# Retention outputs and gate kept with channels on partitions in a two-layer transformer kernel

## The reference

```python
xh = x.reshape(B, S, HEADS, HEAD)                 # 16, 256, 8, 16; x is the normalised input
q, k, v = (einsum('bshd,hde->bshe', xh, W) for W in (Wq, Wk, Wv))
scores = einsum('bnhd,bmhd->bhnm', q, k) * D[None]     # causal decay
ret = einsum('bhnm,bmhd->bnhd', scores, v)
mu, var = mean(ret, axis=-1), var(ret, axis=-1)        # over the 16 channels of a head
ret = (ret - mu) * rsqrt(var + EPS)
ret = ret.reshape(B, S, HIDDEN) * gn_w + gn_b
gated = x @ W1
out = (gated * sigmoid(gated) + ret) @ W2
```

## Time and profile before

| what | us |
|---|---|
| median of 3 runs (770.76 to 773.18) | 770.95 |
| the profiled execution | 769.98 |
| its span, first to last instruction | 768.1 |
| PE busy in it | 704.7 (92%) |
| DVE busy | 547.3 (71%) |
| ACT busy | 419.5 (55%) |
| POOL busy | 327.5 (43%) |

### The profile page before, as it was taken

One profiled execution on the slowest core, in us unless ns is written; L12 is line 12 of the kernel. 1 busy time (PEld: TensorE's weight loads), 2 busy tenths in 40 slices (PEclk: granted clock), 3 DMA queues, 4 the chain that ended last, 5 costly groups with the idle time before them and its releaser, 6 DMA issues.

```text
span 768.1 us, 17690 instructions
## 1 busy us (share of the span) xinstructions
PE 704.7 (92%) x6133; PEld 526.7 (69%) x6133; DVE 547.3 (71%) x1053; ACT 419.5 (55%) x802; POOL 327.5 (43%) x433
## 2 busy tenths in 40 slices
PE   5787788998899978979898999999999999999997
PEld 4643445556755537756666888888888888888885
DVE  6878997885688856779886766666666666666665
ACT  5745665776577768667664444444444444444442
POOL 3765644783758860147694641212122222222222
PEclk9999999999999999999999999999999999999999
DMA  6974655431144420011113511112121211211100
GB/s 190 265 231 140 174 149 199 152 103 43 54 127 125 131 84 1 9 36 57 57 44 117 152 55 55 55 41 67 42 68 42 66 43 53 56 51 59 41 15 14
DMA packets 63796, 66.51 MB, mean 87 GB/s; under 512 B 6513, under 2 KB 41841, under 8 KB 63729
## 3 DMA queue, kind: packets, MB, share of 16 engines
q1 hardware_dynamic: 62128, 63.23, 27.5%
q0 software_dynamic: 1024, 2.12, 1.1%
q10 hardware_dynamic: 576, 0.27, 0.1%
HBM read 47.46 MB, written 17.99 MB: 85 GB/s over the span
## 4 chain that ended last, share of the span: by engine, by line
PE 75%; DVE 10%; ACT 5%; issue 4%; DMA 3%; POOL 2%; SPq 0%; ACTq 0%; POOLq 0%; DVEq 0%
PE ps L1763 25%; PE ps L1992 22%; DVE m L1241 3%; PE ps L1876 3%; PE ps L1683 3%; PE ps L1587 3%; DMA qk_parts<-qk_p 2%; PE ps L1796 2%; PE ps L1831 2%; PE ps L1597 2%; PE ps L1593 2%; PE ps L1897 1%; PE ps L1601 1%; PE ps L1688 1%; PE ps L1580 1%
## 5 line engine op out<-in xcount | busy, mean ns | idle before, releaser
L963 ACT ACTIVATE f_h<-ps 128x512 fp32r<-128x512 f32 x256 | 153.3, 599 | 197.7 <-PE ps L1763 197.7
L1463 DVE SCALAR_TENSOR_TENSOR f_l<-ps,f_h 128x512 fp32r<-128x512 f32 x256 | 175.9, 691 | 112.5 <-ACT f_h L963 111.3
L1763 PE MATMUL ps<-x_hl,w_h 128*128 (+1 forms) x512 | 200.3, 391 | 0.0
L783 POOL TENSOR_TENSOR acc<-acc,yt 128x512 f32<-128x512 f32 x55 | 70.9, 1289 | 249.8 <-DVE yt L1501 249.8
L877 ACT ACTIVATE probs<-ps 128x1536 f32<-128x1536 f32 x64 | 92.8, 1450 | 33.9 <-PE ps L1606 33.3
L1763 PEld LDWEIGHTS ps<-x_hl,w_h 128*128 128x128 f32 x512 | 96.1, 188 | 19.6
L682 POOL TENSOR_SCALAR_AFFINE_SELECT probs<-probs 128x512 f32<-128x512 f32 x128 | 78.4, 637 | 59.9 <-ACT probs L877 59.6
L1992 PE MATMUL ps<-f_l,w_h 128*128 128x512 f32 x256 | 99.8, 390 | 1.4 <-DVE f_l L1463 1.4
L1992 PE MATMUL ps<-f_h,w_h 128*128 128x512 f32 x256 | 99.7, 390 | 0.0
L1763 PE MATMUL ps<-x_hl,w_l 128*128 (+1 forms) x256 | 99.6, 389 | 0.0
L1992 PE MATMUL ps<-f_h,w_l 128*128 128x512 f32 x256 | 99.6, 389 | 0.0
(11 more groups left out here) (225 smaller groups left out, 1329.5 us busy)
## 6 DMA issues: line engine op xcount, KB each, us to landing
gate_b<-gate_rows SPq DMA_DIRECT2D x64, 256.0 KB, 3.3
qk_parts<-qk_p SPq DMA_DIRECT2D x16, 512.0 KB, 3.9
k_st<-qk_parts SPq DMA_DIRECT2D x64, 96.0 KB
q_st<-qk_parts SPq DMA_DIRECT2D x64, 96.0 KB
y_tok<-zero SPq DMA_DIRECT2D x8, 512.0 KB, 2.7
w_raw<-in_w_e SPq DMA_DIRECT2D x16, 256.0 KB, 2.8
x_rows<-xn_rows SPq DMA_DIRECT2D x8, 260.0 KB, 4.2
w_up<-in_w_up SPq DMA_DIRECT2D x8, 256.0 KB, 2.9
```

Of the source, the lines that this page charges most:

```text
L783: nc.gpsimd.tensor_tensor(acc[:, :], acc[:, :], yt[:, e % 2, :], ALU.add).then_inc(summed, 1)
L963: nc.scalar.activation(r32(f_h[:, m % 4, :]), ps[:, m % 4, :], ACT.Relu).then_inc(f_hi, 1)
L1463: nc.vector.scalar_tensor_tensor(out=r32(f_l[:, m % 4, :]), in0=ps[:, m % 4, :], scalar=0.0, in1=f_h[:, m % 4, :], op0=ALU.max, op1=ALU.su ...
L1763: last = nc.tensor.matmul(dst, r32(lhs[i]), r32(rhs[j]), start=(k == 0), stop=(k == 2))
```

## The change

Retention outputs stay with channels on partitions all the way from the weighing to W2. ACT makes squares and a copy straight from `ps_o1`. PE sums the squares of a head by a product with a constant 128x128 matrix `same_head` (one where two channels share a head), which leaves each sum in all 16 channels of its head, so root and inverse now run on 128x256. DVE multiplies `o1` by `gn_w` (now one number per partition) and by the inverse in one instruction; POOL adds `sg` and writes `zT`. The transpositions, `ret`, `ss1`, `z`, `put_heads`, `put_turned` and `square_sums` go. For this the gate must have channels on partitions too: in `products` the token-major product shrinks from 264 to 136 columns and a new one, with the gate weights stationary and 256 token columns moving, is added. POOL adds `gn_b` to `sg` once, in 16 instructions. `ps_at1` moves to bank 7. `add_retention` goes ahead of the masks in DVE's step, ACT's root moves between its two score copies, `project1` comes a step earlier (s-3), and the sum of squares of s-2 stands behind the scores. One more constant is loaded at the start (64 KB) and `gn_w` is smaller.

```diff
...
 def ps_qk1(u): return ps[:, 2 + u, :]
-def ps_p1(u, t): return ps[:, 4 + 2 * u + t, 0:PROJ1]
-def p1_both(u): return ps[:, 4 + 2 * u:6 + 2 * u, 0:PROJ1]
+def ps_p1(u): return ps[:, 4 + 2 * u, 0:TB * (D + E)].rearrange("p (t c) -> p t c", t=TB)
+def ps_g1(u): return ps[:, 5 + 2 * u, 0:S]
 ps_o1 = ps[:, 6, 0:S]
-ps_at1 = ps[:, 6, S:2 * S]
-ps_r1 = ps[:, 7, 0:S]
-ps_zt = ps[:, 7, S:2 * S]
+ps_at1 = ps[:, 7, S:2 * S]
+ps_ss1 = ps[:, 7, 0:S]
 EARLY, LATE = slice(0, NT * 3 // 4), slice(NT * 3 // 4, NT)
...
         last.then_inc(v1_here, 1)
+    for b in range(B):
+        pool.wait_ge(sg_put, b + 1)
+        nc.gpsimd.tensor_tensor(sg[:, b, :], sg[:, b, :], gn_b[:, 0:1].broadcast_to([P, S]), ALU.add).then_inc(sg_biased, 1)
     pool.wait_ge(lg1_put, B + CREDIT)
-    pool.wait_ge(sg_put, B)
...
             pool.wait_ge(z_a, b)
-            tiles = z[:, (b - 1) % 2, :, :]
-            nc.gpsimd.tensor_tensor(tiles, tiles, gn_w[:, :].unsqueeze(1).broadcast_to([P, TB, D]), ALU.mult).then_inc(z_b, 1)
-            pool.wait_ge(z_b, b)
-            nc.gpsimd.tensor_tensor(tiles, tiles, sg[:, (b - 1) * TB:b * TB, :], ALU.add).then_inc(z_done, 1)
+            pool.wait_ge(sg_biased, B)
+            if b >= 3:
+                pool.wait_ge(wo_mm, B + b - 2)
+            nc.gpsimd.tensor_tensor(zT[:, (b - 1) % 2, :], o1[:, (b - 1) % 2, :], sg[:, b - 1, :], ALU.add).then_inc(z_done, 1)
         if b % 2 == 1 and b + 1 < B:
...
         act.wait_ge(p1_mm, b + 1 + CREDIT)
-        nc.scalar.activation(sg[:, ds(b * TB, TB), :], p1_both(u)[:, :, D + E:PROJ1], ACT.Silu).then_inc(sg_put, 1)
+        nc.scalar.activation(sg[:, ds(b, 1), :].rearrange("p o t -> p (o t)"), ps_g1(u), ACT.Silu).then_inc(sg_put, 1)
         if isinstance(b, int) and b == 3:
...
         if b >= 1:
-            act.wait_ge(turned1, b)
-        nc.scalar.activation(o1[:, :], ps_o1, ACT.Copy).then_inc(o1_evac, 1)
+            act.wait_ge(squared, b)
+        if b >= 2:
+            act.wait_ge(z_done, b - 1)
+        nc.scalar.activation(sq[:, :], ps_o1, ACT.Square)
+        nc.scalar.activation(o1[:, b % 2, :], ps_o1, ACT.Copy).then_inc(o1_evac, 1)
     def deviation_of(b):
-        act.wait_ge(ss_done, b + 1)
+        act.wait_ge(squared, b + 1)
         if b >= 2:
             act.wait_ge(rden_done, b - 1)
-        nc.scalar.activation(sd1[:, b % 2, :, :], ss1[:, b % 2, :, :], ACT.Sqrt, bias=eps[:, 0:1], scale=1.0 / HD1).then_inc(sd_done, 1)
-    def put_heads(b):
-        act.wait_ge(turned1, b + 1)
-        if b >= 2:
-            act.wait_ge(z_a, b - 1)
-        nc.scalar.activation(ret[:, b % 2, :, :].rearrange("p t c -> p (t c)"), ps_r1, ACT.Copy)
-        if b >= 1:
-            act.wait_ge(ss_done, b)
-        nc.scalar.activation(sq[:, :, :].rearrange("p t c -> p (t c)"), ps_r1, ACT.Square).then_inc(ret_put, 1)
-    def put_turned(b):
-        act.wait_ge(zt_mm, b + 1)
-        act.wait_ge(turned1, min(b + 3, B))
-        if b >= 2:
-            act.wait_ge(wo_mm, B + b - 1)
-        nc.scalar.activation(zT[:, b % 2, :], ps_zt, ACT.Identity, bias=gn_b[:, 0:1]).then_inc(zt_put, 1)
+        nc.scalar.activation(sd1[:, b % 2, :], ps_ss1, ACT.Sqrt, bias=eps[:, 0:1], scale=1.0 / HD1).then_inc(sd_done, 1)
...
                 nc.scalar.activation(sc[:, i % 3, :, 2 * P:3 * P].rearrange("p (c x) t -> p c x t", x=2), rectangle(i % 2), ACT.Copy).then_inc(copied, 1)
+                if i == 2 * s and s >= 2:
+                    deviation_of(s - 2)
+        elif s - 2 < B:
+            deviation_of(s - 2)
         if s + 1 < B:
             evacuate1(s - 1)
-        if 0 <= s - 2 < B:
-            deviation_of(s - 2)
         if s == B + 2:
             hidden_unit(0, 1)
-        if 0 <= s - 1 < B:
-            put_heads(s - 1)
-        if 0 <= s - 3 < B:
-            put_turned(s - 3)
         if s == 1:
...
                                 gam[:, :, :], ALU.mult).then_inc(qk1_put, 1)
-        dve.wait_ge(sg_put, b + 1)
-        nc.vector.tensor_copy(v1[:, ds(b * TB, TB), :], p1_both(u)[:, :, 0:D + E]).then_inc(lg1_put, 1)
+        dve.wait_ge(p1_mm, b + 1 + CREDIT)
+        nc.vector.tensor_copy(v1[:, ds(b * TB, TB), :], ps_p1(u)).then_inc(lg1_put, 1)
         if more(b, 2):
...
             dve.wait_ge(z_a, b)
-        if b >= 2:
-            dve.wait_ge(zt_mm, b - 1)
-        nc.vector.reciprocal(rs1[:, b % 2, :, :], sd1[:, b % 2, :, :]).then_inc(rden_done, 1)
+        nc.vector.reciprocal(rs1[:, :], sd1[:, b % 2, :]).then_inc(rden_done, 1)
         dve.wait_ge(rden_done, b + 1)
-        nc.vector.tensor_tensor(z[:, b % 2, :, :].rearrange("p t (h d) -> p t h d", h=H1),
-                                ret[:, b % 2, :, :].rearrange("p t (h d) -> p t h d", h=H1),
-                                rs1[:, b % 2, :, :].unsqueeze(3).broadcast_to([P, TB, H1, HD1]), ALU.mult).then_inc(z_a, 1)
+        nc.vector.scalar_tensor_tensor(out=o1[:, b % 2, :], in0=o1[:, b % 2, :], scalar=gn_w[:, 0:1], in1=rs1[:, :], op0=ALU.mult, op1=ALU.mult)\
+          .then_inc(z_a, 1)
-    def square_sums(b):
-        dve.wait_ge(ret_put, b + 1)
-        if b >= 2:
-            dve.wait_ge(sd_done, b - 1)
-        nc.vector.tensor_reduce(ss1[:, b % 2, :, :], sq[:, :, :].rearrange("p t (h d) -> p t h d", h=H1), AX.X, ALU.add).then_inc(ss_done, 1)
     def heads_step(s):
+        if s == B + 3:
+            split_unit(0, 1)
+        if 0 <= s - 4 < B:
+            add_retention(s - 4)
         if s < B:
...
             normalise_heads(s - 2)
-        if s == B + 3:
-            split_unit(0, 1)
-        if 0 <= s - 4 < B:
-            add_retention(s - 4)
         if s == 0:
...
             sum_before(s - (B - 5))
-        if 0 <= s - 1 < B:
-            square_sums(s - 1)
         if s == B - 1:
...
             pe.wait_ge(x_attn, B)
+        if b >= 2:
+            pe.wait_ge(sg_put, b - 1)
         for t in range(TB):
-            last = three(ps_p1(u, t), [x_[:, t * P:(t + 1) * P] for x_ in rhs], [w[:, :] for w in w1_p])
-        last.then_inc(p1_mm, 1)
+            three(ps_p1(u)[:, t, :], [x_[:, t * P:(t + 1) * P] for x_ in rhs], [w[:, 0:D + E] for w in w1_p])
+        three(ps_g1(u), [w[:, D + E:PROJ1] for w in w1_p], rhs).then_inc(p1_mm, 1)
     def find_slots():
...
                 pe.wait_ge(o1_evac, s)
-            if s >= 4:
-                pe.wait_ge(x_attn, B + s - 3)
         for h in range(GH):
...
-    def turn1(b):
+    def sum_squares(b):
         pe.wait_ge(o1_evac, b + 1)
         if b >= 1:
-            pe.wait_ge(ret_put, b)
-        for t in range(TB):
-            last = nc.tensor.transpose(ps_r1[:, t * P:(t + 1) * P], o1[:, t * P:(t + 1) * P], ident[:, :])
-        last.then_inc(turned1, 1)
-    def turn_z(b):
+            pe.wait_ge(sd_done, b)
+        if b >= 2:
+            pe.wait_ge(x_attn, B + b - 1)
+        nc.tensor.matmul(ps_ss1, same_head[:, :], sq[:, :], start=True, stop=True).then_inc(squared, 1)
+    def project1(b):
         pe.wait_ge(z_done, b + 1)
-        if b >= 1:
-            pe.wait_ge(zt_put, b)
-        pe.wait_ge(ret_put, min(b + 2, B))
-        for t in range(TB):
-            last = nc.tensor.transpose(ps_zt[:, t * P:(t + 1) * P], z[:, b % 2, t, :], ident[:, :])
-        last.then_inc(zt_mm, 1)
-    def project1(b):
-        pe.wait_ge(zt_put, b + 1)
-        pe.wait_ge(o1_evac, min(b + 4, B))
+        pe.wait_ge(sd_done, min(b + 2, B))
         if b >= 1:
             pe.wait_ge(x_attn, B + b)
-        if b >= B - 2:
-            pe.wait_ge(gt_put, 1)
         for t in range(TB):
+    pe.wait_ge(late_in, (LATE_IN + 2) * 16)
+    pe.wait_ge(sg_put, B)
     pe.wait_ge(lg1_put, B + CREDIT)
...
             pe.wait_ge(gates_done, PARTS + 2)
-            pe.wait_ge(x_attn, 2 * B - 2)
+            pe.wait_ge(o1_evac, B)
             for c in range(2):
             last.then_inc(gt_mm, 1)
+        if 0 <= s - 2 < B:
+            sum_squares(s - 2)
         if 0 <= s - 1 < B:
         if 0 <= s - 3 < B:
-            turn_z(s - 3)
-        if 0 <= s - 1 < B:
-            turn1(s - 1)
-        if 0 <= s - 4 < B:
-            project1(s - 4)
+            project1(s - 3)
     run_steps(step)
...
 "w2_a": i["L1_attn_W2"],
-"gn_w": rows(i["L1_attn_gn_w"]),
+"gn_w": np.ascontiguousarray(i["L1_attn_gn_w"][:, None]),
 "gn_b": np.ascontiguousarray(i["L1_attn_gn_b"][:, None]),
 "gam": gam.astype(np.float32),
+"same_head": (at[:, None] // HD1 == at[None, :] // HD1).astype(np.float32),
 "odd_rows": (at[:, None] // HD1 % 2).astype(np.float32),
...
```

26 lines of the change are left out of this document (13 added, 13 removed).

## The result

The changed kernel takes 798.71 us (median of 4 runs, 796.44 to 798.8) beside 772.07 for the kernel before in the same session: a ratio of 1.0327, 95% interval 1.031 to 1.0345. That is 26.6 us more, where I had said 13.1 (784.0, range 777.5 to 790). The direction was right and the size was half of what came.

A forecast was written before the change was run, and what follows sets the result against it. DVE was taken as the bound from mask 3 to mask 15, PE in the projection. 3.6 - 0.6 + 10.1 + 0 = +13.1 us on the profiled 769.98 gave 783.1, as a median 784.0; 80% range 777.5 to 790.

The forecast's parts named there:

- The length of the inverse: DVE's reciprocal in the retention steps, growing from 16 to 256 elements: 1.79 us, 1.54 more, at 6.4 ns an element.
- The estimate of 2.25: Inverse on DVE read as eight cycles of 0.96 GHz per element: 2.25 us, making the sum 5.5 us higher.
- DVE's part, +10.1: Mask 3 to mask 15: twelve longer inverses add 18.5 us, less 4.8 for `square_sums` and 3.6 of waiting.
- POOL's disturbance: DVE's scaling might be slowed while POOL is busy: up to 4.8 us, put into the range only.
- So DVE should never wait between mask 3 and mask 15: Retention stage: the other loops fit within DVE's late step of 4.91 us, so DVE runs without waiting.
- three loops: Retention steps, checked against 4.9 us: PE's work, scores to masks, and ACT's root to the inverse.
- Moving `add_retention` ahead of the masks costs nothing: DVE's retention step: the product the addition needs was issued at the end of PE's step before; cost nothing.
- What PE and ACT lose: Retention steps: fewer transpositions and copies, a new product of 0.45 us; engines would wait for DVE, so counted as nothing.
- Steps 0 to 3, -0.6: First retention steps: earlier scores and no `square_sums`, against a longer first inverse: -0.6 us, between 0 and -1.2.
- Projection, +3.6: Projection stage: +0.31 us a sequence from short products with own weight loads, 13 sequences, less 0.4 at the end.
- The end, 0: After mask 15: gates leave at about the same distance and PE's wait covers the third inverse: 0, between -0.5 and +1.5.
- PE's clock: Retention stage rival: DVE waits for PE only if a PE step passes 4.9 us; a few us, chance 0.03.

The follow-up runs named there:

- a5_add_after_masks: Changed kernel with DVE's addition to x moved behind the masks, one sequence earlier, ahead of the inverse: 786.91 us, ratio 1.0182.
- the second profile: The changed kernel run once more, unchanged, beside other kernels on one chip: 798.15 us, ratio 1.0333 to the kernel before.
- a7_own_bank: Changed kernel with the sums of squares in the upper half of the weighing result's bank, on a slower chip: 808.1 us, ratio 1.0248.
- c1_old_projection: Changed kernel with the old projection of six 264-column products a sequence, the gate in the wrong layout: 796.24 us, ratio 1.0293.
- b1_old_split_columns: Kernel before with each 264-column product made as one of 136 and one of 128 columns, on a slower chip: 793.73 us, ratio 1.0079.
- a3_short_inverse: Changed kernel with the reciprocal on only 16 of its 256 elements, the rest set to 1 once: 781.38 us, ratio 1.0102.
- a6_both: Changed kernel with the reciprocal on 16 of 256 elements and DVE's addition behind the masks: 776.49 us, ratio 1.0043.
- p2_root_and_inverse_on_act: Changed kernel with DVE's addition behind the masks and ACT taking root and inverse in one operation, on a slower chip: 787.94 us, ratio 1.0006.
- b2_old_with_inverse: Kernel before with one more reciprocal of 256 elements per sequence on DVE, on a slower chip: 809.67 us, ratio 1.0286.
- p4_single_pass_squares: Changed kernel with addition behind masks, root and inverse in one ACT operation, and the sum-of-squares product in rounded format: 769.54 us, ratio 0.9948.

## Why the prediction was right or wrong

**The length of the inverse** (1.79 us, from the slope of three small sizes): right, 1.743. The longest base, 6.4 ns for each element, was the one to take; 16 to 256 elements gives (1743 - 250) / 240 = 6.2 ns. The estimate of 2.25 that I had drawn from the page "VectorE: DVE Perf Modes" of the Trainium skill (First, the fixed hardware budget) is refuted by that row: a repeat count of eight is not eight cycles of 0.96 GHz for each element.

**DVE's part, +10.1**: right. a5_add_after_masks, with the same work on DVE and no bank wait, measured +9.6, and late steps of 4.78 and 5.23 for my 4.91 and 5.4. The scaling took 0.48 for 0.42; of the 4.8 us that I had kept in the range for POOL's disturbance no more than that came. The comparisons beside POOL did not cost more in sum either (10.1 us in the stage, 10.4 before).

**"So DVE should never wait between mask 3 and mask 15"**: wrong, and this is the step that failed; it is worth 9.0 us of the 26 (7.5 by the second profile): DVE waited 9.3 us there, in twelve steps of twelve. I had checked three loops for it, scores to masks, ACT's root to the inverse, and the length of PE's work. The fourth was in the diff: `pe.wait_ge(x_attn, B + b - 1)` ahead of the sum of squares, and the sum ahead of the weighing. "Moving `add_retention` ahead of the masks costs nothing" looked at what the addition waits for, not at who waits for the addition. Put behind the long inverse of the step before, it reached PE 1.75 us later, with the weighings queued behind. The rule of the Trainium skill that bears on it is in "PSUM — Partial Sum Buffer" (PSUM bank collisions raise a hardware error): two engines may not access one bank in the same quadrant at once, whatever the address, so the order must be made by semaphores. The wait in the code is that rule's price, and the 17.8 us of PE's waiting show it in the trace; a7_own_bank, in which the sums have another bank, does without it, and its late steps are free of DVE's wait.

**What PE and ACT lose "I cost at nothing"**: wrong, though small beside the rest. The product that I put at 0.45 measured 0.63 to 0.67. In the changed kernel it is a piece of the chain above, between DVE's addition and the weighing that DVE's mask waits for, and it mattered again as soon as the inverse was gone.

**Steps 0 to 3, -0.6**: the number is right, -0.7; its three parts were not measured apart.

**Projection, +3.6**: the price of a product was right, the sum too high. Fifteen products took 1.74 for 1.43, the +0.31 forecast:

```profile
297.62 0.22 PE ps L1732 x2
297.83 1.74 PE ps L1738 x15
```

But the pair of transpositions between two chains shrank from 0.37 to 0.22, so that a sequence grew by about 0.15 only, 2.5 us in all (c1_old_projection), 3.2 where PE's clock fell as well. That 3.2 lies near the 3.6 forecast is luck. I had taken the twelve products' 1.43 from the chain and left the 0.37 beside it out. In b1_old_split_columns the pair shrank too (0.24), in the old layout, so it goes with the short products or the longer chain ahead of it; which of the two, no run tells. The Trainium skill's formula for an isolated matmul ("TensorE: Matmul & The Clock Gate", Back-to-back issue gap) would have made it level; b1_old_split_columns (0.106 us for each short product) shows that with a load for each product it does not apply, as that page itself warns.

**The end, 0**: wrong, +4.8. The step that failed is the claim that the gates leave at about the same distance, as PE comes to them late anyway, and that PE's 1.40 us of wait covers the third inverse. These are the chain's pieces, for the earlier trace rows, and below them a row of DVE's timeline:

```profile
433.95 0.04 DVE gates L1462
...
436.07 1.76 DVE rs L1371
...
440.87 1.26 POOL w_l L764
442.13 4.76 DMA w_raw<-in_w_e
...
448.00 0.50 PE ps L1956
```

```profile
430.43 1.75 DVE L1371 RECIPROCAL rs<-sd 128x256 f32<-128x256 f32 x1 [1.88 <-ACT sd L986]
```

The gates came 11.5 us after mask 15, not 9.5, because DVE stood for 1.88 us waiting for ACT's root, which waits for the sum, which waits for the addition: the same link, with the sum at 1.21 us for 0.67 where PE was granted 0.50 (428.5 to 431.9). Then the third inverse (436.07) held DVE, POOL's split and the load behind it, and PE's first wait in the expert stage ended 25.6 us after mask 15 where it had been 20.8; from there to the end both kernels took 348.9. The same distance is 23.4 without the link (a5_add_after_masks, in which PE did not wait there), 22.0 without the long inverse (a3_short_inverse), 21.6 without either (a6_both) and 20.3 in p2_root_and_inverse_on_act; in the old order the long inverse alone made it 26.9 (b2_old_with_inverse). So inverse and link both carry it, and together they cost more than each alone; these are single profiles. I had seen this chain and priced its slack from the row of PE's wait, 1.40, without adding up the three inverses on it.

**The sum**: of the 12.9 us between +26.0 and the +13.1 forecast, 8.5 are the retention stage (18.6 for 10.1) and 4.8 the end; projection and steps 0 to 3 take back 0.5.

**PE's clock**, given 0.03 and "a few us": I had said that DVE waits for PE only if a step of PE passes 4.9. With the link through the bank PE is in the loop at any length. The two profiles of the changed kernel differ by 1.5 us in the stage, with 11.9 and 10.2 us of it at the lower level; how much of the loss is the clock's, no run separates.

**The range** held DVE's own uncertainty (the slope, POOL's disturbance, the comparisons: up to 9 us above) and no new wait at all. A rival of that kind, with its place and a price, was missing.

## What to carry to other kernels

When an instruction is moved behind a long one on its engine, ask who waits for it, and what is queued behind the waiter: here 1.75 us on DVE reached DVE again by way of an addition, a product and a weighing on PE. Two tiles in one PSUM bank are one resource between engines; list every wait that their sharing makes before calling a loop free. When a stretch of a profile is longer than expected, look first at the clock that PE was granted in it: 3 to 7 us at 1.2 GHz behind mask 15 went with 1.6 to 2.9 us more in a6_both, b2_old_with_inverse and p4_single_pass_squares. And an operation that costs several nanoseconds an element belongs where the elements are few (16 sums of squares a token), or into an instruction that is issued anyway, as ACT's root.
